# Window-attention scores on sixteen 32x32 tiles, heads through the ring banks, and one layer's rows normalised on ScalarE

## The reference

```
def attn_a(x):   # 16 heads of 8, 2 key/value heads, windows of 32
    q = (x @ Wq + bq) ...; k, v = ... repeated 8 times
    # block n of 32 queries sees 64 keys: half a block before it to half a block behind
    scores = einsum('bhntd,bhnud->bhntu', qb, kb)
    scores = where((u >= t) & (u < t + 32), scores, -inf)
    out = einsum('bhntu,bhnud->bhntd', softmax(scores), vb)
    return out @ Wo + bo
def ffn(x):      # 128 -> 512, butterfly of 9 stages, gelu, butterfly, 512 -> 128
    return butterfly(gelu(butterfly(x @ W_exp + b_exp, up) + up_bias), down) @ W_con + b_con + down_bias
def attn_b(x):   # linear attention over each sequence, elu(x) + 1 features
    ...
x = x + attn_a(ln(x)); x = x + ffn(ln(x)); x = x + attn_b(ln(x)); x = x + ffn(ln(x))
```

## Time and profile before

| what | us |
|---|---|
| median of 3 runs | 546.74 (546.36 to 548.43) |
| the profiled execution, its own time | 548.77 |
| its span, from the first instruction to the last | 547.0 |
| PE busy in the span | 514.8 (94%) |
| POOL / DVE / ACT busy | 449.6 / 424.4 / 356.5 |

### The profile page before, as it was taken

How to read it: one execution, slowest core, us unless ns; L and a number is a source line. 1 busy time by engine, 2 the same in 40 slices (tenths; PEclk the granted TensorE clock), 3 DMA queues, 4 the chain that set the end, 5 groups by cost and what they waited for, 6 DMA issues and landing times.

```text
span 547.0 us, 14353 instructions
## 1 busy us (share of the span) xinstructions
PE 514.8 (94%) x5060; PEld 337.4 (62%) x5060; DVE 424.4 (78%) x1272; ACT 356.5 (65%) x578; POOL 449.6 (82%) x640
## 2 busy tenths in 40 slices
PE   4788989999999999999999999999999999999996
PEld 2454344756667676666676676766576676767764
DVE  4978888997978888887888888888878687745451
ACT  2654457576768777776767686776777777747542
POOL 6548789999989999898998989999979796797240
PEclk9999999999999999999999999999999999999999
DMA  8433323231322212131423222231422312110001
GB/s 305 153 100 85 101 63 84 59 79 46 103 50 79 60 46 76 43 102 38 103 50 105 49 59 74 61 85 40 118 64 63 72 27 59 31 29 20 1 20 40
DMA packets 49543, 38.87 MB, mean 71 GB/s; under 512 B 12352, under 2 KB 38976, under 8 KB 49472
## 3 DMA queue, kind: packets, MB, share of 16 engines
q1 hardware_dynamic: 47024, 33.73, 24.4%
q10 hardware_dynamic: 2448, 4.22, 2.2%
HBM read 15.64 MB, written 5.51 MB: 39 GB/s over the span
## 4 chain that ended last, share of the span: by engine, by line
PE 61%; POOL 19%; DVE 5%; issue 5%; DMA 5%; SPq 3%; ACT 2%; POOLq 0%; DVEq 0%; ACTq 0%
PE ring L785 15%; PE ring L773 14%; POOL probs_t L602 7%; PE ring L715 6%; PE ps_s L741 6%; PE ring L796 4%; PE ps_o L758 4%; PE ring L816 3%; PE ring L866 2%; DMA probs_t<-probs_t 2%; SPq L446 2%; PE ring L843 2%; PE ring L805 1%; DMA x_P<-in_x 1%; POOL xb_W L572 1%
## 5 line engine op out<-in xcount | busy, mean ns | idle before, releaser
L602 POOL TENSOR_TENSOR probs_t<-probs_t,first 128x1024 f32<-128x1024 f32 x64 | 151.4, 2376 | 19.3 <-DMA probs_t<-probs_t 19.1
L785 PEld LDWEIGHTS ring<-w,early 128*128 128x128 f32 x1024 | 118.9, 192 | 10.8 <-issue 8.5
L1189 ACT ACTIVATE early<-ring,b 128x512 f32<-128x512 f32 x128 | 84.3, 685 | 62.2 <-PE ring L773 61.8
L785 PE MATMUL ring<-w,early 128*128 128x128 f32 x1024 | 119.8, 275 | 1.8 <-ACT early L1189 1.6
L1180 ACT ACT_TABLE_LOAD x58 | 74.4, 1283 | 10.1 <-issue 9.1
L1198 ACT ACTIVATE probs_t<-merged_t 128x1024 f32<-128x1024 f32 x64 | 65.8, 1044 | 11.4 <-DVE merged_t L1547 9.3
L741 PE MATMUL ps_s<-kx,q_t 64*32 64x512 f32 x960 | 64.7, 596 | 2.9 <-DVE merged L1540 1.6
L1555 DVE STREAM_TRANSPOSE ps_o<-ps_o 128x512 f32<-128x512 f32 x64 | 46.1, 721 | 21.3 <-PE ps_o L758 21.3
L773 PE MATMUL ring<-xT_G,w1b 128*128 128x512 f32 x128 | 60.8, 595 | 0.7 <-ACT xT_G L1170 0.7
L773 PE MATMUL ring<-xT_F,w1b 128*128 128x512 f32 x128 | 60.1, 608 | 0.4 <-ACT xT_F L1170 0.3
L1528 DVE COPY_PREDICATED ps_s<-first,ps_s 128x512 f32<-128x512 uint32 x64 | 43.9, 687 | 15.9 <-PE ps_s L741 14.7
(11 more groups left out here) (124 smaller groups left out, 985.7 us busy)
## 6 DMA issues: line engine op xcount, KB each, us to landing
probs_t<-probs_t SPq DMA_DIRECT2D x256, 64.0 KB, 2.0
kx<-kv_rows SPq DMA_DIRECT2D x120, 40.0 KB, 2.1
x_P<-in_x SPq DMA_DIRECT2D x16, 256.0 KB, 3.3
out_x<-x_G SPq DMA_DIRECT2D x16, 256.0 KB, 2.5
vx_t<-kv_rows SPq DMA_DIRECT2D x128, 8.0 KB
up_s<-in_up_m ACTq DMA_DIRECT2D x7, 256.0 KB, 7.9
down_s<-in_down_m ACTq DMA_DIRECT2D x7, 256.0 KB, 8.1
kv_rows<-kv_t SPq DMA_DIRECT2D x16, 80.0 KB, 2.8
```

Of the source, the lines that this page charges most:

```text
L602: nc.gpsimd.tensor_tensor(parts, parts, keep.rearrange("p (a t) -> p a t", a=1).to_broadcast([P, PAIR * HEADS, WIN]), ALU.mult).then_inc(p ...
L785: last = nc.tensor.matmul(bank(name)[:, P * j:P * (j + 1)], hid[s][:, c, P * j:P * (j + 1)], w2[:, c], start=(c == 0), stop=(c == CH - 1))
L1189: nc.scalar.activation(hid[s][:, c], bank(name)[:], ACT.Gelu, bias=b1[:, c:c + 1]).then_inc(drained[BANK[name]].sem, 1)
```

## The change

Scores: HG = 4 heads instead of 8 share the rows of a tile, so the contraction has 32 rows, and a tile j takes sixteen matmuls of 32 by 32 with 256 columns. The four row groups write four banks, so `ps_s` has four, of which half of each is used. The order of the query columns (`query_order`, `key_rows`) follows, `kx` halves, and `first_keys_out` has four instructions instead of eight.

Values: `ps_o` is gone. The two key/value heads of a tile go to two ring banks (PRODUCTS names pairs: "32", "10", "23", "12"), so a values tile waits for two banks. `heads_turned` transposes into SBUF (`o_raw`) and frees the first bank; `sums_inverted` writes the inverses into the second bank; `heads_divided` frees that.

L's rows: GpSimd makes scale and shift (`row_scales`), ScalarE applies them (`normalise`, four activations), for all groups.

Order: all tables and all `turn` functions are new. Butterfly stages stand before group 0's first transpose on TensorE, the down-stage before its moments on VectorE, the diagonals before its variance on GpSimd, the clearing of `kx` after it. A group goes from P.xT to G.down in six turns instead of seven. The mask and softmax steps keep their instructions.

```diff
+HG = HPK // 2
+ROWS = HEADS // HG
...
-        ps_s = ctx.enter_context(nc.psum_tensor("ps_s", [P, 2, 512], F32))
-        ps_o = ctx.enter_context(nc.psum_tensor("ps_o", [P, 2, 512], F32))
-        ring = [ctx.enter_context(nc.psum_tensor(f"ring{i}", [P, 512], F32)) for i in range(4)]
+        ps_s = ctx.enter_context(nc.psum_tensor("ps_s", [P, ROWS, 512], F32))
+        ring = ctx.enter_context(nc.psum_tensor("ring", [P, 4, 512], F32))
...
+        def head_banks(j):
+
+            lo, hi = sorted(int(b) for b in BANK[f"W.PV{j}"])
+            return ring[:, lo:hi + 1:hi - lo, 0:HPK * WIN]
...
-                own = drained[BANK[name]]
-                if (name, "bank") not in COVERED:
-                    pe.wait_ge(own.sem, own.after(g, name) - own.unit)
+                for b in BANK[name]:
+                    if (name, f"bank {b}") not in COVERED:
+                        pe.wait_ge(drained[b].sem, drained[b].after(g, name) - drained[b].unit)
...
+                keys = kx_0 if g == 0 else kx
                 for i in range(4):
-                    for a in range(KV):
-                        half, c = slice(HPK * HD * a, HPK * HD * (a + 1)), WINDOW[a][i]
-                        keys = kx_0 if g == 0 else kx
+                    for r in range(ROWS):
+                        rows, c = slice(HG * HD * r, HG * HD * (r + 1)), WINDOW[r % KV][i]
                         last = nc.tensor.matmul(
-                            ps_s[32 * i:32 * i + 32, a], q_t[half, P * j + 32 * c:P * j + 32 * c + 32],
-                            keys[half, :, TSPAN * j + 32 * c:TSPAN * j + 32 * c + SPAN],
+                            ps_s[32 * i:32 * i + 32, r % KV * (ROWS // KV) + r // KV, 0:HG * SPAN], q_t[rows, P * j + 32 * c:P * j + 32 * c + 32],
+                            keys[rows, :, TSPAN * j + 32 * c:TSPAN * j + 32 * c + SPAN],
                             start=True, stop=True)
...
-                            last = nc.tensor.matmul(ps_o[32 * c:32 * c + 32, a, 0:HPK * WIN], vx[rows, j, a, s],
+                            last = nc.tensor.matmul(head_banks(j)[32 * c:32 * c + 32, a], vx[rows, j, a, s],
...
+            def normalise(g, s):
+
+                act.wait_ge(rooted.sem, rooted.after(g, f"{s}.nmr"))
+                act.wait_ge(product.sem, product.after(g - 1, TURNED[s]))
+                for j in range(TILES):
+                    last = nc.scalar.activation(xn[s][:, j], x_of(g, s)[:, j], ACT.Identity, bias=nmr[s][:, j:j + 1],
+                                                scale=rstd[s][:, j:j + 1])
+                last.then_inc(scaled.sem, 1)
...
-                nc.vector.transpose(ps_o[:, :, 0:HPK * WIN], ps_o[:, :, 0:HPK * WIN]).then_inc(vec.sem, 1)
+                earlier = f"W.PV{(j - 2) % 4}"
+                divided = drained[BANK[earlier][1]]
+                dve.wait_ge(divided.sem, divided.after(g if j >= 2 else g - 1, earlier))
+                nc.vector.transpose(o_raw[:, j % 2], head_banks(j)).then_inc(first_bank.sem, 1)
...
+                nc.vector.reciprocal(sum_inverses(j), o_raw[:, j % 2].rearrange("p k (h r) -> p k h r", h=HPK)[:, :, :, HD:HD + 1]
+                                     ).then_inc(vec.sem, 1)
```

More of the change, by code:

```diff
@@ L171 @@
+TURNS = NG + 103
 CHUNKS = {"a": [0, 1], "b": [2, 3]}
 COVERED = {
[L173 to L177 removed]
@@ L178 @@
-    ("P.kv", "P.xT"), ("P.q", "P.xT"), ("W.PV1", "values"), ("W.PV2", "values"), ("W.PV3", "values"),
-    ("W.S0", "X.ka"), ("W.S1", "P.q"), ("W.S1", "X.ka"), ("W.S1", "keys"), ("W.S2", "P.q"), ("W.S2", "X.kb"),
-    ("W.S2", "keys"), ("W.S3", "P.q"), ("W.S3", "X.kb"), ("W.S3", "keys"), ("W.proj", "bank"), ("X.d0", "bank"),
-    ("X.d1", "X.d0"), ("X.d2", "X.d1"), ("X.d2", "bank"), ("X.d3", "bank"), ("X.d4", "X.d3"), ("X.d5", "bank"),
-    ("X.d6", "bank"), ("X.ka", "bank"), ("X.kb", "P.xT"), ("X.u0a", "bank"), ("X.u0b", "bank"), ("X.u1a", "X.u0a"),
[3 rows of a table removed]
+    ("F.down", "F.up1"), ("F.down", "F.up2"), ("F.down", "F.up3"), ("F.down", "X.d6"), ("F.down", "bank 1"),
[4 rows of a table added]
@@ L186 @@
+    ("L.out1", "L.kv"), ("L.out1", "L.q"), ("L.q", "L.xT"), ("P.q", "P.xT"), ("W.PV0", "bank 2"), ("W.PV1", "values"),
[8 rows of a table added]
+    ("X.wT", "X.u6b"), ("X.wT", "bank 3"),
 }
 SCORES = ["W.S0", "W.S1", "W.S2", "W.S3"]
+LAST_DIVIDED = "W.PV3"
 WEIGHTED = ["W.PV0", "W.PV1", "W.PV2", "W.PV3"]
@@ L804, in linear_q @@
                 free(g, "L.q")
-                nc.tensor.matmul(bank("L.q")[:], wl_s[:, 0:P], x_t["L"][:], start=True, stop=True
+                nc.tensor.matmul(bank("L.q"), wl_s[:, 0:P], x_t["L"][:], start=True, stop=True
                                  ).then_inc(product.sem, 1)
@@ L842, in attention_q @@
                 free(g, "P.q")
-                nc.tensor.matmul(bank("P.q")[:], wq_s[:], x_t["P"], start=True, stop=True
+                nc.tensor.matmul(bank("P.q"), wq_s[:], x_t["P"], start=True, stop=True
                                  ).then_inc(product.sem, 1)
@@ new lines, in turn @@
+                for g in due(t, -1, 13):
+                    scores(g, 2)
+                if t == 14:
+                    weighted_values(14, 2)
+                for g in due(t, 1, 1, 12):
+                    ffn_up(g, "F", 1)
+                for g in due(t, 1, 0, 13):
+                    ffn_up(g, "F", 2)
+                if t == 1:
+                    ffn_up(0, "F", 3)
+                    ffn_up(0, "F", 0)
+                for g in due(t, 2, 0, 12):
+                    linear_state(g)
@@ L1149, in _ @@
             for n in range(2):
-                last = nc.tensor.matmul(ring[3][:], d_tmp[:, 0], d_tmp[:].rearrange("p c n -> p (c n)"), start=True, stop=True)
+                last = nc.tensor.matmul(ring[:, 3], d_tmp[:, 0], d_tmp[:].rearrange("p c n -> p (c n)"), start=True, stop=True)
             last.then_inc(warmed, 1)
@@ new lines, in turn @@
+                for g in due(t, 2, 2, 12):
+                    residual(g, "F", "F.down", "W")
+                if t == 13:
+                    subtract_max(13, 3)
+                if t == 4:
+                    linear_divided(1, 1)
+                for g in due(t, 2, 0, 1):
+                    residual(g, "F", "F.down", "W")
+                    moments(g, "F")
+                for g in due(t, 1, 1, 12):
+                    heads_turned(g, 3)
+                if t == 12:
+                    merge_halves(13, 0)
@@ new lines, in turn @@
+                for g in due(t, 2, 13, 14):
+                    residual(g, "F", "F.down", "W")
+                for g in due(t, 2, 2, 14):
+                    moments(g, "F")
+                if t == 16:
+                    heads_turned(15, 3)
+                for g in due(t, 2, 0, 1):
+                    moments_joined(g, "F")
+                for g in due(t, 1, 1, 12):
+                    sums_inverted(g, 3)
+                for g in due(t, 2, 13, 14):
+                    moments_joined(g, "F")
@@ new lines, in turn @@
+                if t == 15:
+                    merge_halves(15, 3)
+                for g in due(t, 0, 1, 12):
+                    values_out(g)
+                if t == 4:
+                    residual(1, "L", "L.proj", "F")
+                for g in due(t, 0, 1, 12):
+                    scores_transposed(g, 3)
+                if t == 4:
+                    moments(1, "L")
+                for g in due(t, -1, 14):
+                    row_max(g, 0)
+                if t == 14:
+                    subtract_max(15, 0)
```

1701 lines of the change are left out of this document (811 added, 890 removed), and 155 rows, old and new, of tables (COVERED, PARTED, PROBS, PRODUCTS).

## The result

The changed kernel takes 555.61 us (median of four runs, 554.44 to 559.15) against 547.42 for the kernel before in four runs beside it: ratio 1.0161, 95% interval 1.0109 to 1.0212. It is slower; 537 was forecast, and the range ended at 550. The profiled execution took 555.29, its span is 553.4, 6.4 us more than the 547.0 of before. The medians differ by 8.2 us: the profiled execution of before (548.77) lies 1.4 us above its median.

The account below looks back on a forecast made before the run. TensorE was taken to bound the kernel from group 2 on, GpSimd next. Terms: -11.2 + 2.0 - 2.0 + 2.8 - 1.4 = -9.8 us, giving a median of 537 us; range 524 to 550.

Parts of the forecast that it names:

- Scores on sixteen tiles: TensorE's score tiles take 0.65 us instead of 1.00; with values pairs 0.80 us saved per group, 11.2 us over 14 groups.
- Two rounds of eight: Rival: sixteen score matmuls on TensorE run as two rounds, 0.95 us a tile, +5.3 instead of -11.2, 553.4 us; chance 0.08.
- The start: Before group 0's first scores: first transpose to about 16.0 us, first scores to 21.1, +2.8; shorter score waits on VectorE, -1.4.
- Heads through the ring: Values tiles in ring banks: TensorE waits some 0.15 us per group for VectorE to free PV1's banks, +2.0 us.
- GpSimd's relief: ScalarE normalises L, GpSimd sheds 1.8 us per group and releases early groups sooner; TensorE idle from 50 to 100 us shrinks, -2.0.
- The last group: Last group's row scales take two more small steps on GpSimd, covered before G.down of group 14 ends: 0, else 0.5 us.
- the rivals on the slower side: TensorE waiting on ring banks VectorE has not divided (557 us, chance 0.09 full, 0.18 mild), and two rounds of eight (0.08).

Follow-up runs that it names:

- e1: Changed kernel with HG = 8 again: eight score tiles of 64x32 into two banks, all else and the order as changed; 575.23 us.
- e2: Changed kernel with group 0's moments, normalisation, transposes, keys and queries ahead of the butterfly stages on every engine; 553.3 us.
- e4: Changed kernel with up_bias_out later on VectorE, X.d4's drain earlier on ScalarE, the first swap of probabilities earlier on SyncE; 556.19 us.
- e13: Changed kernel with the start reordered on each engine: group 0's transposes first, its attention drawn together, group 2's entry and group 1's scores drawn forward; 547.26 us.
- e8: Changed kernel with one pair swapped on TensorE in groups 2 to 12, values tile ahead of score tile, so F.up follows a score tile; 562.76 us.
- e7: Changed kernel with the ScalarE part undone: GpSimd normalises L rows of groups 0 to 14, VectorE those of the last; 557.38 us.
- e6: Changed kernel with the last group's L rows normalised on VectorE again, ScalarE keeping the other groups'; 555.86 us.
- e9: Changed kernel with twenty unread identity matmuls put into TensorE's empty stretches at the start; 555.52 us.
- e15: e13's kernel with X.wT behind group 0's projection and group 2's queries, and butterfly stages u6 and d3 ahead of group 1's first score tile; 548.94 us.

## Why the prediction was wrong

**Scores on sixteen tiles: right, and even low.** 0.65 a tile was forecast; 0.65, 0.71, 0.70 and 0.66 were measured. The four pairs with the extra change took 5.15 us for the 5.05 to 5.07 forecast, a gain of 0.72 for 0.80. Two rounds of eight (the rival at 553.4) did not happen, although the total came near it. e1 puts the tiles' whole worth at some 19 us, since the start gains by them too.

**The term that was missing: the order in the steady turn.** The sum let everything outside the pairs stand, and saw only one change of tiling more. e1 shows 0.74 us a period for the order, so that of 1.10 gained 0.36 stayed. F.up had four banks in a row before; with the values in the ring it has three, goes in two halves with the linear state and a pair between, and starts behind a 64x32 tile.

**The step that failed: the start.** It was put at "the first scores move from 18.35 to about 21.1", +2.8, with -1.4 against it, +1.4 in all; up to F.xT of group 0 it cost +10.8. The first scores moved by 4.6. The first transpose came at 17.66 and not at 16.0: the 5.38 us copied from before hold 1.20 for the rows of group 0 on VectorE, and these now took 2.65, beside the clearing of `kx` that the new order had put there. Worse, I ended the account at the first scores and let the rest follow at a fixed distance. It doesn't: from there to F.xT the delay went from 4.6 to 10.8, through the values behind `up_bias_out`, the bank held for X.d4, X.wT ahead of W.oT, and x and keys of group 2 that are loaded late. In the traces no single one moves F.xT by more than the 1.3 us of chance (e2 to e4), since another of like height stands beside it, though by the medians group 0's rows first (e2) are worth some 3 us; together, in e13, they are 8.75. The last 2 us, and how much of the whole is the half clock, are not resolved.

**Heads through the ring: +2.0 forecast, 0 in the steady state.** TensorE has no gap there. The bank was nearly as tight as computed, though: with one pair swapped it waits 0.45 us (e8). At the start, ring banks take part in two of the waits (d4 in the changed kernel, d5 in e4).

**GpSimd's relief: -2.0 forecast, 0.** The 2 us were idle of TensorE between 50 and 100 us; e7 gives the work back to GpSimd, and neither that idle time (7.6 us, 8.0 in e7) nor the period changes by much. One activation took 482 ns where I took 310.

**The last group: 0 forecast, +3.0.** 0.6 us are busy time of TensorE, 2.4 idle. It is not ScalarE's rows of the last group (e6), nor of any (e7). It stands at 50.6 or 50.7 us in every run, e1 and e13 too; the closing order was not tried, and the cause stays open.

**The sum.** Forecast: -9.8. Measured: +10.8 - 7.4 + 3.0 = +6.4 in the profiled executions, +8.2 in the medians. Of the rivals on the slower side neither came; one that followed group 0 to the second turn through the new order was not among them.

## What to carry to other kernels

When a change rewrites the order, follow the first group through each engine's queue to the end of its first turn; a delay at the first product says little about that at the tenth. Waits in a start stand side by side, so a single repair tests nothing but itself; repair all that the last trace shows and read the next. And a gain on one operation should be tried with the rest of the change in place, as well as the rest without it: here some 19 us won and 27 lost (eight tiles in the new order, 575.23, against 548.17) stood behind a difference of 8.

## What the runs showed of the hardware

**VectorE beside GpSimd.** VectorE's normalisation of group 0, four instructions of 128x128 from SBUF to SBUF, took 1.12 us in e13, with no GpSimd work beside it. It took 2.65 in the changed kernel, beside the memset of `kx` (2.23), 4.98 in e1, beside one of 4.37, and 3.50 in e2, beside the diagonals. The rows of e1, VectorE's and GpSimd's timeline:

```profile
15.11 4.98 DVE L1488 TENSOR_SCALAR xn_P<-x_P,mv_P,rstd_P 128x128 f32<-128x128 f32 x4
```

```profile
14.94 4.37 POOL L543 MEMSET kx<- 128x5120 f32 x1
```

VectorE stands for as long as GpSimd's instruction lasts, and then does its own: in e1 its first instruction, 0.35 us in e13, lasts 4.27, to 19.38, and the memset ends at 19.31. The Trainium skill says so in "SBUF — State Buffer", section SBUF: two separate sides: the port pair that the two share is locked for a whole instruction and not divided. These rows agree, for a memset too, which reads nothing.

**The clock and empty stretches.** TensorE fell to the 1.2 GHz level within or right behind idle times of 3.24 us (changed kernel), 2.28 (e9) and 2.40 (e15), and the kernel before, whose longest idle time between 20 and 62 us is 1.30 us, kept 2.4 GHz there. One idle time alone doesn't decide it, either way: in the kernel before one of 2.28 us, ending at 17.77, left the clock up, and in e4 the clock fell at 45.8 us, where no idle time from 27 us on is longer than 1.25:

```profile
43.02 0.73 PE L760 MATMUL ps_s<-kx,q_t 32*32 32x256 f32 x32 [1.25 <-DVE merged L1527]
44.83 0.67 PE L777 MATMUL ring<-probs_t,vx 64*32 64x256 f32 x16 [1.08 <-POOL probs_t L617]
46.62 1.17 PE L760 MATMUL ps_s<-kx,q_t 32*32 32x256 f32 x32 [1.13 <-DVE merged L1527]
```

```profile
40.00:45.70 5.70, 3.16 (x88) 1.56 (x88) 5.27 (x10) 2.05 (x3) 3.06 (x2) 1.00 0.43 111
45.80:62.80 17.00, 11.61 (x120) 5.30 (x121) 12.67 (x39) 3.76 (x5) 10.37 (x14) 0.50 0.34 86
```

At the lower level four transposes took 1.09 to 1.11 us for 0.66, and X.wT, which ran partly there, 5.54 for 3.70.
